# Low parts and split maxima on another engine, and the steps in another order, in a three-part decoder layer

## What is computed

```python
x = _layernorm(x + _L0_attn_ref(x, ...))            # 16 heads of 8, with relative positions
x = _layernorm(x + _L0_xattn_ref(x, ctx, ctx, ...)) # 16 heads of 8, causal
x = _layernorm(x + _L0_ffn_ref(x, ...))             # one shared expert, 8 experts, top 2

attn1 = jnp.einsum('bhqd,bhkd->bhqk', q, k)
attn2 = jnp.einsum('bhqd,qkd->bhqk', q, rk2)
attn = jax.nn.softmax((attn1 + attn2) / scale, axis=-1)
w1 = jnp.einsum('bhqk,bhkd->bhqd', attn, v)
w2 = jnp.einsum('bhqk,qkd->bhqd', attn, rv2)

h1 = jax.nn.gelu(jnp.einsum('td,edh->teh', flat, rw1) + rb1[None], approximate=False)
expert_out = jnp.einsum('teh,ehd->ted', h1, rw2) + rb2[None]
mixed = jnp.einsum('ted,te->td', expert_out, weights)
```

## Time and profile before

| | us |
|---|---|
| median of 3 runs | 483.2 |
| lowest and highest | 480.25, 483.86 |
| the profiled execution | 484.97 |
| its span | 482.9 |

### The profile page before, as it was taken

The page is one execution under the profiler, slowest core; times in us unless marked ns, Lnnn a source line. Parts: engine busy times, 40 slices in busy tenths (PEclk is TensorE's granted clock), DMA queues, the critical chain, the costliest instruction groups (busy, mean ns, idle before and its releaser), DMA issues.

```text
span 482.9 us, 11287 instructions
## 1 busy us (share of the span) xinstructions
PE 406.3 (84%) x4718; PEld 302.9 (63%) x4729; DVE 324.4 (67%) x630; ACT 248.0 (51%) x329; POOL 76.4 (16%) x84
## 2 busy tenths in 40 slices
PE   3775399847879999999899899998999998649992
PEld 2464158734656877767688676776786767525772
DVE  4429953698868787887787868888975377143233
ACT  2470187703558583368774932487973425514340
POOL 9700000201340120003411100113101102410000
PEclk9776589959999999999999999999999999876998
DMA  4558025140013513001121630011110200000001
GB/s 107 156 113 261 3 68 155 35 121 5 3 36 88 175 47 99 3 18 44 37 68 23 166 99 1 4 36 24 49 24 1 81 20 3 2 23 0 2 0 23
DMA packets 29324, 26.87 MB, mean 56 GB/s; under 512 B 12577, under 2 KB 27866, under 8 KB 28506
## 3 DMA queue, kind: packets, MB, share of 16 engines
q1 hardware_dynamic: 28442, 26.02, 20.0%
q10 hardware_dynamic: 832, 0.13, 0.2%
...
## 4 chain that ended last, share of the span: by engine, by line
PE 55%; DVE 22%; ACT 8%; DMA 5%; issue 4%; SPq 4%; POOL 1%; POOLq 0%; DVEq 0%; ACTq 0%
PE ps_f L708 12%; PE ps_f L719 11%; PE ps_s L545 8%; PE ps_f L571 5%; PE ps_f L671 3%; DVE ST L930 3%; DVE ST L960 3%; DMA QS<-MP 3%; PE ps_f L579 2%; ACT ST L786 2%; DVE MX L933 2%; PE ps_s L538 2%; PE ps_f L518 2%; PE ps_f L524 2%; SPq L414 2%
## 5 line engine op out<-in xcount | busy, mean ns | idle before, releaser
L545 PE MATMUL ps_s<-QS,KS 125*128 125x128 bf16 (+1 forms) x768 | 80.6, 249 | 16.7 <-DVE ST L930 11.2
L545 PEld LDWEIGHTS ps_s<-QS,KS 125*128 125x128 bf16 (+1 forms) x768 | 64.4, 106 | 43.9 <-issue 14.9
L833 ACT ACTIVATE HT<-ps_f,hb 128x512 f32<-128x512 f32 x72 | 48.9, 689 | 81.5 <-PE ps_f L708 39.2
L719 PEld LDWEIGHTS ps_f<-w,HT 128*128 128x128 f32 x576 | 69.2, 192 | 10.0 <-issue 7.4
L708 PE MATMUL ps_f<-x2T,w 128*128 128x512 f32 x144 | 73.5, 619 | 0.0
L719 PE MATMUL ps_f<-w,HT 128*128 128x128 f32 x576 | 73.3, 278 | 0.0
L790 ACT ACTIVATE ST<-ST 128x1024 f32<-128x1024 f32 x32 | 33.6, 1060 | 52.1 <-DVE ST L960 51.7
L1044 DVE SCALAR_TENSOR_TENSOR acc<-ps_f,gw,acc 128x128 f32<-128x128 f32 x128 | 37.4, 363 | 31.3 <-PE ps_f L719 31.2
L483 POOL TENSOR_SCALAR_AFFINE_SELECT PC<-PC 128x1024 f32<-128x1024 f32 x32 | 34.8, 1096 | 147.8 <-ACT PC L797 147.7
L930 DVE TENSOR_TENSOR ST<-ps_s,ST 128x1024 f32<-128x1024 f32 x32 | 38.6, 1207 | 13.4 <-PE ps_s L545 13.4
L937 DVE TRANSPOSE_TENSOR_REDUCE MX<-ps_s 128x32 f32<-128x1024 f32 x32 | 39.0, 1237 | 7.1 <-PE ps_s L545 7.1
...
## 6 DMA issues: line engine op xcount, KB each, us to landing
...
QS<-parts_by_head SPq DMA_DIRECT2D x24, 256.0 KB, 3.8
KS<-parts_by_head SPq DMA_DIRECT2D x24, 256.0 KB, 4.9
...
cin<-in_ctx SPq DMA_DIRECT2D x4, 256.0 KB, 4.5
...
QS<-MP SPq DMA_DIRECT2D x48, 8.0 KB, 2.1
```

The lines of the kernel that those rows point to most:

```text
L545: last = nc.tensor.matmul(ps[:, o:o + S], KS[a][0:kd, c:c + S], queries(a, kd, h, j), start=not masked and j == 0, stop=j == NB - 1, skip_ ...
L719: last = nc.tensor.matmul(ps[:, b * E:(b + 1) * E], HT[n % 2][:, f, b * S:(b + 1) * S], w2[:, e, f, :], start=f == 0, stop=f == NF - 1 and ...
L833: nc.scalar.activation(HT[n % 2][:, f, :], ps[:, :], ACT.Gelu, bias=hb[:, e, f:f + 1]).then_inc(ht_ready, 1)
```

## The change

Three things change. The low part of q, k, ck and cq is computed by GpSimd and no longer by VectorE; the wait for the middle part goes with it. The four instructions that split the negated maxima are GpSimd's too; VectorE keeps the maximum itself, and from the second chunk on waits there for an earlier split, so that it doesn't write over what is still read. And `SCHEDULE` has the same 488 steps in another order, of which the diff shows the first line.

```diff
@@ SCHEDULE
-0load 1load 0xT 0q 0v 0k 0cT 0loadc 0st_q 0st_k 1xT 0ck 1q 0bias.0 0cv 0bias.1 0bias.2 0bias.3 0bias.4 0bias.5
+0cT 0load 0cv 0loadc 0xT 0q 0ck 0st_q 0v 0k 0bias.0 0bias.1 0bias.2 1load 0bias.3 0bias.4 0bias.5 0bias.6 1loadc
...
@@ gpsimd
             for ch, what, t in ORDER:
-                if what in ("xT", "x1T"):
+                if what in SLOT:
+
+                    i = min(SLOT[what], 2)
+                    k = int(what in ("k", "ck"))
+                    g.wait_ge(mid_ready[what], ch + 1)
+                    nc.gpsimd.tensor_tensor(part[i][:, LOW, :], rest[k][:, :], part[i][:, MID, :],
+                                            ALU.subtract).then_inc(low_ready[what], 1)
+                elif what in ("m", "cm"):
+
+                    a = int(what == "cm")
+                    n = 2 * ch + t
+                    g.wait_ge(negmax[a], n + 1)
+                    if ch:
+                        g.wait_ge(shifted[a][t], 16 * NSH * ch)
+                    nc.gpsimd.tensor_copy(MP[a][:, 0, t, :], NM[a][:, t, :]).then_inc(mp_step[a], 1)
+                    g.wait_ge(mp_step[a], 4 * n + 1)
+                    nc.gpsimd.tensor_tensor(NR[a][:, t, :], NM[a][:, t, :], MP[a][:, 0, t, :], ALU.subtract).then_inc(mp_step[a], 1)
+                    g.wait_ge(mp_step[a], 4 * n + 2)
+                    nc.gpsimd.tensor_copy(MP[a][:, 1, t, :], NR[a][:, t, :]).then_inc(mp_step[a], 1)
+                    g.wait_ge(mp_step[a], 4 * n + 3)
+                    nc.gpsimd.tensor_tensor(MP[a][:, 2, t, :], NR[a][:, t, :], MP[a][:, 1, t, :], ALU.subtract).then_inc(mp_step[a], 1)
+                elif what in ("xT", "x1T"):
@@ vector
-                    v.wait_ge(mid_ready[what], ch + 1)
-                    nc.vector.tensor_tensor(part[i][:, LOW, :], rest[k][:, :], part[i][:, MID, :],
-                                            ALU.subtract).then_inc(low_ready[what], 1)
@@ vector
                     n = 2 * ch + t
+                    if ch:
+                        v.wait_ge(mp_step[a], 4 * (n - 1))
                     nc.vector.tensor_reduce(NM[a][:, t, :], ps[:, 0:P].rearrange("p (a i) -> p i a", a=NQ),
                                             AXIS.X, ALU.max, negate=True).then_inc(negmax[a], 1)
-                    v.wait_ge(negmax[a], n + 1)
-                    if ch:
-                        v.wait_ge(shifted[a][t], 16 * NSH * ch)
-                    nc.vector.tensor_copy(MP[a][:, 0, t, :], NM[a][:, t, :]).then_inc(mp_step[a], 1)
...
```

More of the change, by code:

```diff
@@ L78 @@
[L78 to L92, removed]
@@ L98 @@
-3cXT 3co 3cln 3x2T 3r 3up.0 3up.1 3up.2 3up.3 3g 3up.4 3dn.0 3up.5 3dn.1 3dn.2 3up.6 3up.7 3up.8 3up.9 3up.10
-3dn.3 3up.11 3dn.4 3up.12 3up.13 3dn.5 3dn.6 3up.14 3up.15 3up.16 3up.17 3dn.7 3dn.8 3fln
+0cT 0load 0cv 0loadc 0xT 0q 0ck 0st_q 0v 0k 0bias.0 0bias.1 0bias.2 1load 0bias.3 0bias.4 0bias.5 0bias.6 1loadc
+0bias.7 0p1.0 0p1.1 1xT 0p1.2 0p1.3 0p1.4 0p1.5 0st_k 0m.0 0p1.6 0p1.7 0p2.0 0m.1 0p2.1 0p2.2 0p2.3 0pv.0 0p2.4
+0pv.1 0st_ck 0p2.5 0pvT.0 0p2.6 0pvT.1 0p2.7 1q 1k 0pv.2 0w2.0 0w2.1 0w2.2 0pv.3 0w2.3 0pvT.2 0pvT.3 0w2T.0
@@ new lines @@
+0w2T.1 0w2T.2 0w2T.3 1st_q 1bias.0 0X 1bias.1 0XT 1bias.2 1bias.3 0o 1bias.4 1bias.5 1bias.6 1bias.7 0ln 1v
+1st_k 2load 1p1.0 0x1T 1cT 0cq 1p1.1 1p1.2 2xT 0st_cq 1p1.3 2q 1p1.4 0c1.0 0c1.1 0c1.2 0c1.3 0c1.4 0cm.0 0c1.5
+0c1.6 1m.0 1ck 1p1.5 0c2.0 0c1.7 0c2.1 0cm.1 1p1.6 0c2.2 0cpv.0 0c2.3 1p2.0 0cpvT.0 1p1.7 0c2.4 0cpv.1 0c2.5
+1p2.1 1m.1 0c2.6 0cpvT.1 2st_q 2loadc 0c2.7 0cpv.2 1p2.2 1pv.0 1p2.3 1p2.4 0cpv.3 1p2.5 1pvT.0 0cpvT.2 1p2.6
+1p2.7 1cv 0cpvT.3 1pv.1 0cX 1pv.2 2k 1w2.0 1pvT.1 1w2.1 0cXT 1pv.3 1w2.2 0co 1st_ck 1pvT.2 1w2.3 2v 1pvT.3 0cln
@@ new lines @@
+1w2T.0 1w2T.1 2bias.0 1w2T.2 0x2T 1w2T.3 2bias.1 1X 0r 2bias.2 1XT 2bias.3 2bias.4 0up.0 1o 2bias.5 0g 0up.1
+2bias.6 2bias.7 2st_k 0up.2 1ln 2p1.0 1x1T 0up.3 1cq 0up.4 2p1.1 2p1.2 0up.5 0dn.0 0dn.1 2p1.3 0dn.2 0up.6 0up.7
+1st_cq 0up.8 1c1.0 1c1.1 0up.9 2m.0 1c1.2 2cT 1c1.3 0up.10 1c1.4 1c1.5 0up.11 2p2.0 1cm.0 0dn.3 2p2.1 1c1.6
+0dn.4 0dn.5 1c2.0 1c2.1 0up.12 1c1.7 2pv.0 2p1.4 0up.13 2p1.5 1cpv.0 2pvT.0 1cm.1 1c2.2 0dn.6 1c2.3 3load 0up.14
+2p1.6 0up.15 0up.16 2p1.7 0up.17 1cpvT.0 1c2.4 2p2.2 0dn.7 2m.1 1cpv.1 1c2.5 2p2.3 0dn.8 1c2.6 1c2.7 1cpv.2 3xT
@@ new lines @@
+1cpvT.1 2p2.4 2p2.5 2cv 1cpv.3 2pv.1 2p2.6 1cpvT.2 2p2.7 1cpvT.3 2pv.2 1cX 3q 2ck 2w2.0 2w2.1 3st_q 2w2.2 2pv.3
+0fln 2pvT.1 1cXT 3v 3k 1co 1cln 2pvT.2 2w2.3 3bias.0 2pvT.3 2w2T.0 3bias.1 2w2T.1 2st_ck 2w2T.2 3loadc 1x2T
+2w2T.3 3bias.2 2X 1r 3st_k 3bias.3 2XT 3bias.4 1up.0 2o 3bias.5 1up.1 3bias.6 3bias.7 2ln 1g 1up.2 3p1.0 2x1T
+1up.3 2cq 3p1.1 1dn.0 1up.4 1up.5 3p1.2 1dn.1 1dn.2 1up.6 3p1.3 1up.7 1up.8 2c1.0 2c1.1 1up.9 2c1.2 2c1.3 2c1.4
+3cT 2st_cq 2cm.0 2c1.5 1up.10 2c1.6 3m.0 1dn.3 2c1.7 2c2.0 1dn.4 2c2.1 1up.11 2cm.1 3p1.4 3p1.5 1up.12 1up.13
@@ new lines @@
+2c2.2 2cpv.0 1dn.5 2c2.3 3p2.0 1dn.6 2c2.4 2c2.5 2cpv.1 2cpvT.0 3p2.1 3p1.6 2cpvT.1 2c2.6 2cpv.2 2c2.7 1up.14
+3p1.7 1up.15 3cv 2cpv.3 1up.16 3m.1 2cX 2cpvT.2 2cpvT.3 1up.17 3p2.2 3p2.3 1dn.7 3pv.0 3p2.4 2cXT 3p2.5 1dn.8
+3pv.1 3p2.6 3pvT.0 3p2.7 3pv.2 2co 3ck 3w2.0 2cln 3pv.3 3pvT.1 3w2.1 2x2T 1fln 3w2.2 2r 2up.0 3w2.3 3pvT.2
+3st_ck 3pvT.3 3w2T.0 3w2T.1 3w2T.2 3w2T.3 2up.1 2up.2 3X 2g 3XT 2up.3 3o 2dn.0 2up.4 3ln 2up.5 2dn.1 3x1T 2up.6
+3cq 2dn.2 2up.7 2up.8 2up.9 2up.10 2dn.3 2up.11 2dn.4 2dn.5 3c1.0 3c1.1 3st_cq 2up.12 2up.13 3c1.2 3c1.3 2up.14
@@ L100 @@
+3c1.4 2up.15 3cm.0 3c1.5 3c1.6 2up.16 3c1.7 2dn.6 2up.17 3cm.1 3c2.0 3c2.1 2dn.7 2dn.8 3c2.2 3c2.3 3cpv.0 3c2.4
+3c2.5 2fln 3cpv.1 3c2.6 3c2.7 3cpv.2 3cpvT.0 3cpvT.1 3cpv.3 3cpvT.2 3cX 3cpvT.3 3cXT 3co 3cln 3x2T 3r 3up.0
+3up.1 3up.2 3up.3 3g 3up.4 3up.5 3dn.0 3dn.1 3up.6 3up.7 3dn.2 3up.8 3up.9 3dn.3 3up.10 3up.11 3dn.4 3dn.5
+3up.12 3up.13 3up.14 3up.15 3up.16 3dn.6 3up.17 3dn.7 3dn.8 3fln
 """
```

15 lines of the change are left out of this document (removed).

## The result

| | before | after |
|---|---|---|
| median of 4 runs each, us | 483.53 | 492.28 |
| lowest and highest | 480.25, 486.51 | 488.94, 493.02 |
| profiled execution, its span | 484.97, 482.9 | 493.02, 490.9 |

What follows compares the result with a forecast made beforehand. TensorE was taken to bound 167 to 366 us, VectorE to set the pace in stretches up to 150 us. 5.5 + 0.8 - 5.4 - 1 - 2 - 2.4 = -4.5 us on 483.2 gave 478.7 us, range 470 to 490.

Steps and rivals of the forecast that it cites:

- The start, +5.5: Up to the first p1: context work now ahead of x delays it from 36.3 to 41.8 us, +5.5 us, covered by nothing later.
- 36 to 107 us, +0.8: First p1 to first c1: a longer shift chain and 1q's product, +0.3, and cq's low part on GpSimd, +0.5 us.
- 107 to 150 us, -5.4: First c1 to the reciprocal of cX: work leaving VectorE gives full relief of 7.7 us, taken at 70%, -5.4 us.
- The four terms that were to win: The gains forecast for 107.3 to 149.8 us (-5.4), 150 to 175 (-1), 167 to 366 (-2) and the tail (-2.4).
- the round trip: Rival: maximum, split, three SP issues and transfer take VectorE's place as the limit, slower, 490 us; chance 0.15.
- 150 to 175, -1: From 150 to 175 us: the set for 1ck is no longer here, -1 us.
- the full stretch, -2: From 167 to 366 us, where TensorE is nearly always busy: 2 of 7 idle us come back, -2 us (0 to -5).
- The tail, -2.4: End of the kernel: 3cm.1 moves ahead of c2.0, so TensorE's 1.87 us shift wait goes, -2.4 us (0 to -3).
- GpSimd's costs: Sixteen low parts and splits on GpSimd, 16 x (1.3 + 1.4) = 43 us, fit beside its 76 us.
- Its mark: Sign of the round trip rival: TensorE's waits for the shift exceed 6 us in the first 165 us.
- Six of the sixteen: Round trip rival's assumption: six of sixteen round trips lie on the path, each growing 1 to 2 us, say 8 us.
- The interface rival: Rival: GpSimd's new 43 us hold VectorE, 0.8 us for perhaps ten meetings, half on the path, +4, so 483; chance 0.06.

Runs made afterwards that it cites:

- three runs: Changed kernel with steps up to 0bias.7 as before: 485.34 us; kernel before with only the new start: 493.37; changed kernel with x, q, v, k ahead of the context: 487.42.
- old start: Steps up to 0bias.7 as in the kernel before, the rest in the changed order: 485.34 us with the changed engines, 483.51 with the engines of before.
- early issue: SP issues each of a shift's three transfers once its part is written, not all after the split: 477.75 us on the kernel before, 482.57 on the changed kernel.

## Why the prediction was wrong, step by step

- **The start, +5.5: right in kind, 1.2 short.** First bias product forecast at 33.25 and found at 33.31, first p1 41.8 and 43.05. The first agreement is better than its parts: the low part ended at 24.70 and not 24.15, and the way from the spread to the bias took 8.6 us and not 9.1. The missing 1.2 us lies behind it: eight bias copies took 8.35 us, from 34.35 to 42.70, where I had put 7.5 at the pace of before (6.52 for seven), and 0.35 pass before VectorE starts. Of the 0.85 us there, 0.6 are waits for TensorE's products at the lower clock, which the forecast had for the first product alone. "What covers it later: nothing" was confirmed by three runs.
- **36 to 107 us, +0.8: it was +2.4.** Up to 0ln it was +2.7 (89.75 and 99.22 us), with +0.3 forecast. The term counted instructions and missed who stands behind whom: q's stack of chunk 1 is issued 42 us behind the first p1 (85.33), where it was 31 before, and the first bias product of chunk 1 runs at 91.45, ahead of 0ln on ScalarE's list. The late 1q isn't the whole reason: with the old start and 1q in its old place the stack still comes 41 us behind, because SP has 1k's spread ahead of it there.
- **107 to 150 us, -5.4: it was -3.9, and not for the reason given.** This is the step that failed, and the later terms rest on it too. It took the time that leaves VectorE (5.5 us of splits and collisions, "leave VectorE", 1.7 for a low part) for time won, at 70%, and set the longer way to the shift against it only once, in the first chunk (0.7 of 1.6 us left). Elsewhere it stood at nothing. The four terms that were to win came to -1.1 us together, where -10.8 was forecast: 9.7 of the 12.5 us between the span forecast and the span measured. In the old order the move gave nothing in this stretch (42.56 against 42.47). The order alone gave 1.9, and 2.8 with the old start; the move on top of it gave 2.0 and 1.3. In the old order VectorE merely exchanged its work for waits. Its own waits in that stretch, engines moved and order old:

```profile
DVE ST L970 <- PE ps_s L575: 7.3, 3, 4.3
DVE MX L955 <- PE ps_s L566: 3.9, 3, 3.0
DVE ST L948 <- PE ps_s L566: 2.2, 2, 1.2
```

That is 13.4 us behind TensorE's products, where the same three had 5.2 before. TensorE in turn waits for shifts. In the new order the round trip did not bind until the splits moved: where the changed kernel's TensorE waits 2.86 us for a shift (at 129.4 us), it waited 1.07 in the same order with the old engines. From the maximum to the third landing are 5.9 us there against 4.5; 0.3 of it is the split on GpSimd, 1.1 a landing of 3.2 us instead of 2.1, whose cause no run isolates.
- **150 to 175, -1, and the full stretch, -2: they were +1.0 and +2.4.** "Of 7 us idle I give 2 back" had no mechanism behind it. From gwT of chunk 0 to gwT of chunk 2 the seven kernels with the splits on GpSimd and no early issue took 191.5 to 195.3 us, the six with them on VectorE 190.0 to 192.3 (one execution each); the changed kernel with the early issue took 187.0. The two groups overlap, but the round trips, longer by 0.4 to 0.6 us on the mean with the splits on GpSimd, and the 5.8 us that the early issue gave here say the same: the few idle us were round trips too.
- **The tail, -2.4: it was -0.6.** The wait for the shift is gone as forecast. The lag behind the kernel before fell from 8.6 us at gwT of chunk 2 to 6.9 at the reciprocal of 3cX, with a new wait of 1.1 us for cq's stack at 3c1.0 in it. Behind that mark 1.1 us came back: TensorE is busy for 43.3 us there and not 42.2 with the same 216 products, at a granted clock of 0.80 and not 0.85.
- **GpSimd's costs: right for the instructions, not for the queue.** Low part 1.16 us (1.27 assumed), split 1.1 in all from 57.74 to 58.87 (1.4 assumed). What a split stands behind came on top: in the old order up to 3.9 us pass from the end of a maximum to the end of its split with both moved to GpSimd, and at most 2.6 on VectorE. VectorE's sum is down by 31 (30 assumed), but 12 of these are the new order's, which takes it from 324.4 to 312.6 us with the old engines; in it 3 of the 64 split instructions are held beside selects, and 9 were before.
- **Of the rivals the round trip came nearest**, at 492 rather than 490, with a chance of 0.15. Its mark, more than 6 us of waits for shifts in the first 165, stood at 9.8, though 5.3 of that had stood in the kernel before under another name. Its mechanism was half seen: I had it decide from 1 us *more* per trip, while with the new engines in the old order the mean trip grew by 0.5, and in the new order by as much. In the old order the trip was already what bound the kernel, and so time taken off VectorE beside it was worth nothing; in the new order it bound again once the splits were on GpSimd. "Six of the sixteen" was an assumption and not a count. That the chain of waits of the kernel before shows just six, 2.1 us of landing each, is luck.
- **The interface rival fell.** It had GpSimd's new work hold VectorE, perhaps ten times for 0.8 us. Beside the sixteen low parts of the changed kernel one instruction of VectorE took longer than others of its kind, by 0.9 us (1.26 and not 0.34, at 360.9), and beside the splits none. GpSimd's 128x512 subtraction itself took 1151 to 1167 ns in all sixteen cases. By the rule of the Trainium skill ("GPSIMD Engine Reference", Performance versus the Vector engine) a low part would, as an estimate, have come out at 1.35 us; measured against VectorE's 0.69 it is 1.67 times, not 2.
